# Gathers of a graph network written out with constant counts and without a wait for their landing

## What is computed

```python
h = jnp.maximum(_layernorm(x, axis=-1), 0.0)
msg_input = jnp.concatenate([h[src], h[dst], edge_attr], axis=-1)
m = jax.nn.relu(msg_input @ Wm1 + bm1)
messages = jax.nn.relu(m @ Wm2 + bm2)
agg = jax.ops.segment_sum(messages, dst, num_segments=N)
u = jax.nn.relu(jnp.concatenate([h, agg], axis=-1) @ Wu1 + bu1)
out = x + h + (u @ Wu2 + bu2)
```

## Time and profile before

| | us |
|---|---|
| median of 3 runs | 946.89 |
| lowest and highest run | 946.84, 947.41 |
| the profiled execution | 952.33 |
| its span (first to last instruction) | 950.6 |
| GpSimd busy in it | 566.0 |
| gathers (L246), 392 of them | 386.1 |

### The profile page before, as it was taken

One profiled execution on the slowest core, in us unless ns is written; L12 is line 12 of the kernel. 1 busy time (PEld: TensorE's weight loads), 2 busy tenths in 40 slices (PEclk: granted clock), 3 DMA queues, 4 the chain that ended last, 5 costly groups with the idle time before them and its releaser, 6 DMA issues. The chain is left out here.

```text
span 950.6 us, 19507 instructions
## 1 busy us (share of the span) xinstructions
PE 751.0 (79%) x3158; PEld 453.1 (48%) x3159; DVE 696.0 (73%) x2407; ACT 608.5 (64%) x1384; POOL 566.0 (60%) x829
## 2 busy tenths in 40 slices
PE   0687768767877778877887776886799999999998
PEld 0344334333433334433443433453457788777776
DVE  3866756666677666776667567766499999998887
ACT  0666556556656565665665566655567788988986
POOL 6656655656566555665556555654198766655453
PEclk9988888889789897889887899988899999999999
DMA  6254445445545455545553454447305799999999
GB/s 158 67 178 158 151 154 175 157 127 178 176 157 168 141 176 165 169 148 161 177 176 129 153 176 155 162 150 232 133 12 176 230 319 335 351 341 349 355 360 328
DMA packets 99726, 184.55 MB, mean 194 GB/s; under 512 B 15101, under 2 KB 16512, under 8 KB 99700
## 3 DMA queue, kind: packets, MB, share of 16 engines
q1 hardware_dynamic: 46084, 80.64, 25.4%
q10 hardware_dynamic: 41072, 77.93, 23.5%
q0 software_dynamic: 12544, 25.72, 10.5%
HBM read 107.25 MB, written 76.98 MB: 194 GB/s over the span
## 5 line engine op out<-in xcount | busy, mean ns | idle before, releaser
L246 POOL DMA_INDIRECT xg<-x_in,ends_now x392 | 386.1, 985 | 142.9 <-issue 130.1
L511 PE MATMUL bank<-ht,w_uh 128*128 128x512 f32 x196 | 146.1, 837 | 114.2 <-ACT ht L441 68.8
L644 POOL TENSOR_TENSOR low<-msgs,high 128x128 fp32r<-128x128 f32 x303 | 152.8, 521 | 73.3 <-ACT high L724 70.1
L309 DVE BATCH_NORM_STATS2 bn<-xg 128x6 f32<-128x128 f32 x392 | 80.6, 278 | 132.4 <-DMA xg<-x_in,ends_now 132.3
L673 DVE TENSOR_SCALAR hot<-node,dst_f,minus_base 128x512 fp32r<-128x512 f32 x229 | 131.2, 616 | 23.2 <-issue 16.3
L777 PE MATMUL bank<-hot,low 128*128 128x512 f32 x303 | 136.4, 450 | 12.2 <-POOL low L644 6.5
L429 ACT ACTIVATE zn<-xn,shift,rstd 128x128 f32<-128x128 f32 x343 | 141.6, 483 | 1.6 <-DVE rstd L348 1.2
L511 PEld LDWEIGHTS bank<-ht,w_uh 128*128 128x128 f32 x196 | 42.6, 249 | 199.6 <-issue 180.1
L436 ACT ACTIVATE ht<-bank 128x512 f32<-128x512 f32 x196 | 109.2, 593 | 30.3 <-PE bank L504 26.1
L778 PE MATMUL bank<-hot,high 128*128 128x512 f32 x303 | 120.8, 399 | 0.0
L504 PE MATMUL bank<-ident,xg 128*128 128x128 f32 x392 | 64.8, 298 | 61.1 <-issue 37.0
(11 more groups left out here) (77 smaller groups left out, 1165.7 us busy)
## 6 DMA issues: line engine op xcount, KB each, us to landing
hu_scratch<-ht ACTq DMA_DIRECT2D x49, 512.0 KB
xh_scratch<-xh_o ACTq DMA_DIRECT2D x49, 512.0 KB
hu_i<-hu_scratch SPq DMA_DIRECT2D x98, 256.0 KB
xh_i<-xh_scratch SPq DMA_DIRECT2D x98, 256.0 KB
out<-xh_o SPq DMA_DIRECT2D x97, 256.0 KB, 4.3
xn<-x_in ACTq DMA_DIRECT2D x44, 512.0 KB
xg<-x_in,ends_now POOLq DMA_INDIRECT x392
edge<-edge_t_in ACTq DMA_DIRECT2D x45, 64.0 KB
```

The source lines that it names most:

```text
L246: pool.indirect_dma_start(xg[:, slot, t, :], None, x, bass.IndirectOffsetOnAxis(ap=ends_now[:, slot8, t:t + 1], axis=0)).then_inc(s_xg[slo ...
L511: pe.matmul(p_hu[:], w_uh[:], ht[:, slot % 2, 2 + n, :], start=True, stop=True).then_inc(s_hus, 1)
L644: return pool.tensor_tensor(low[:, at, :], msgs[:, k, :], high[:, at, :].bitcast(F32), ALU.subtract)
```

## The change

The loop over the steps on GpSimd becomes 49 steps written out, so that every wait has a constant count and every gather reads its eight index columns straight from `ends_all`. The ring `ends_now`, its copies and their semaphore are gone. Of the three waits of a step one is left, for the transposes of the slot's last user, with the same count as before (4(s - 3) - 2 = 4(s - 4) + 2). The wait for the landing of the step before is gone. Instead, each gather posts `s_made` when GpSimd has written its descriptors (`engine_sem`), and gather n waits for that of gather n - 3 (`AHEAD = 3`).

```diff
--- before.py
+++ after.py
@@ -24,6 +24,7 @@
 EPS = 1e-5
 STAT = 12
 TABLE = 18
+AHEAD = 3
 assert GROUPS == 2 * STEPS and (NEW - LAST) % 4 == 0
 
 
@@ -92,7 +93,7 @@
         s_rng = sem("ranges_moved")
         s_xn = [sem(f"nodes_loaded{i}") for i in range(4)]
         s_xg = [sem(f"ends_gathered{i}") for i in range(4)]
-        s_cp = sem("ends_copied")
+        s_made = sem("gathers_issued")
         s_stat = sem("stat")
         s_sd = sem("sd_ready")
         s_zv = sem("z_by_vector")
@@ -133,7 +134,6 @@
         with ExitStack() as one:
             ident = sb("ident", [P, P], on=one)
             ends_all = sb("ends_all", [P, STEPS, 8], I32, on=one)
-            ends_now = sb("ends_now", [P, 8, 8], I32, on=one)
             dst_i = sb("dst_i", [P, ET + SPARE], I32, on=one)
             minus_i = sb("minus_i", [P, GROUPS], I32, on=one)
 
@@ -227,31 +227,24 @@
                 pool.memset(ident[:], 0.0).then_inc(s_cst, 1)
                 pool.memset(msgs[:, ET:, :], 0.0).then_inc(s_cst, 1)
                 pool.wait_ge(s_idx, 16)
-                pool.tensor_copy(ends_now[:, 0:4], ends_all[:, 0:4, :]).then_inc(s_cp, 1)
-                pool.wait_ge(s_cp, 1)
-
-                def body(s, slot8, use8):
-                    slot = slot8 % 4
-                    if at_least(s, 4):
-                        pool.wait_ge(s_tr, 4 * (s - 3) - 2)
-                    if at_least(s, 1):
-
-                        pool.wait_ge(s_xg[(slot8 - 1) % 4], 128 * (2 * use8 + (slot8 - 1) // 4 + 1))
-                    if at_least(s, 4):
-                        pool.wait_ge(s_cp, 8 * use8 + slot8 - 2)
-                    if below(s, STEPS - 4):
-                        pool.tensor_copy(ends_now[:, (slot8 + 4) % 8, :], ends_all[:, s + 4, :]
-                                         if isinstance(s, int) else ends_all[:, bass.ds(s + 4, 1), :]).then_inc(s_cp, 1)
+
+                for s in range(STEPS):
+                    slot, use = s % 4, s // 4
+                    if s >= 4:
+                        pool.wait_ge(s_tr, 4 * (s - 4) + 2)
                     for t in range(8):
+                        n = 8 * s + t
+                        if n >= AHEAD:
+
+                            pool.wait_ge(s_made, n - AHEAD + 1)
                         pool.indirect_dma_start(
                             xg[:, slot, t, :], None, x,
-                            bass.IndirectOffsetOnAxis(ap=ends_now[:, slot8, t:t + 1], axis=0)).then_inc(s_xg[slot], 16)
-                    if not at_least(s, 1):
+                            bass.IndirectOffsetOnAxis(ap=ends_all[:, s, t:t + 1], axis=0), engine_sem=s_made
+                            ).then_inc(s_xg[slot], 16)
+                    if s == 0:
                         pool.wait_ge(s_cst, 6)
                         pool.affine_select(out=ident[:], in_=ident[:], compare_op=ALU.not_equal, fill=1.0, base=0,
                                            pattern=[[-1, P]], channel_multiplier=1).then_inc(s_cst, 1)
-
-                run_steps(pool, STEPS, 8, STEPS - 4, 8, body)
 
             def start_table(dve, did):
```

## The result

The changed kernel took 977.63 us (median of 4 runs, 973.80 to 985.41) beside 947.15 us for the kernel before: 1.033 times the time, 95% interval 1.0267 to 1.0395. Forecast were 939.9 us and a range of 929 to 960. The profiled execution took 976.8 us, span 975.1.

The account below looks back on a forecast made before the run. The loop through ScalarE's second relu, the node load's issue and L320 was taken to set the step's length in stage one. Terms -3.1 - 14.1 + 10.2 = -7.0 us gave 946.9 - 7.0 = 939.9 us, range 929 to 960.

Parts of the forecast that it names:

- No wait for landing: GpSimd's gathers no longer wait for the previous step's landing: start gains 3.1 us, seven long steps 14.1 us.
- the slower rival: From L174's issue to L320, each node load slows by 1.0 us a step: +22.8, 969.7 us; chance 0.15.
- The seven long steps: Steps that gathers end, L309 running straight into L320; expected to fall back to the load's 4.0 us: -14.1 us.
- The gathers at the load's start: Gather bursts move to the node load's issue; one gather delays each of some 40 loads by 0.255 us: +10.2 us.
- The new wait: On GpSimd, each gather waits for the descriptors of gather n - 3; priced at zero.
- the straight code: GpSimd's loop written out; a late instruction fetch costs some us once, with four steps of cover: priced at zero.
- the indices: Indices read in place: 45 copies of 187 ns leave GpSimd; priced at zero, 8.4 us together without cover.
- gathers bind: Within a rival: waits costing over 0.3 us on GpSimd; every 0.1 us more is 39 us; chance 0.08 shared with another case.
- 3.2 us "to spare": GpSimd's slack per step: eight gathers take 10.3 us of a 13.5 us step.
- Even sharing of the DMA engines: Rival: engines serve gather and load queues in turn, +0.5 us a step on the load: +2.8, 949.7 us; chance 0.15.

Follow-up runs that it names:

- the one with two slots: Changed kernel, but gathers wait for the transposes of step s - 2 instead of s - 4: 910.2 us (chip 6), 904.0 (chip 0), 963.8 (chip 14).

## Why the prediction was wrong

**The step that failed is "No wait for landing".** It priced the start at -3.1 us. On the first chip it was +23.7 (step 3 at 82.38 instead of 58.70). I asked what the wait holds up, and found two idle stretches of L309. I did not ask what the wait keeps apart: it was also the only break in GpSimd's issue, and on such chips VectorE and TensorE need one. The trace of before had a hint: signals some tenths of a us late at the end of its runs. Neither the sum nor any rival held such a case; the slower rival put the loss in the node loads, of which none became slow.

**The terms in the steady part were about right against the trace they were read from.** The seven long steps went: none of 42 loads takes over 4.6 us to L313, against seven before, worth about 14 us. The gathers at the load's start cost 4.14 - 3.99 = 0.15 us each, 6 us in all, against 0.255 and 10.2 forecast. But a third term was missing: ScalarE's second relu starts 9.22 us after L313 instead of 9.01, since the transposes wait 1.31 us for their input's signal instead of 0.53; over 44 steps that is 9 us. -14 + 6 + 9 = +1, as measured between the two profiled executions. The -14 itself was partly luck of that trace: it was read from an execution 5.4 us over the median and applied to the median too, and with the landing wait put back one step was long, not seven, and the steady part 9 us shorter. The new wait, the straight code (21 instruction packets) and the indices cost nothing, as priced; that was shown by putting back the landing wait alone.

**What the late signals cost in all** is seen between chips, in the same kernel: step 48 starts at 687.4 us on the first and 614.2 on chip 0. Of these 73 us, 27 stand before step 3, and 46 after it, 1.0 us a step, of which the second relu (it starts 9.22 against 8.28 us after L313) has 0.94. That the rest of the two chips is alike is assumed here.

**Where no signal is late, the sign was right and the size was not.** The start gained 3.2 us (58.27 to 55.10) for 3.1 forecast. Yet the gain is 63 us, not 7, because there gathers end 31 of 42 steps in the kernel before, not seven: a step falls from 13.84 to 12.46 us. In the forecast that stood only as "gathers bind", for another reason. That a trace of one chip says seven and of another thirty-one could not be read from the one at hand; that the margin was thin could: eight gathers of 10.1 us, 2.4 of landing and 0.9 to the next start are 13.4, against a step of 13.5. I had called 3.2 us "to spare" without setting the landing against it.

**Even sharing of the DMA engines** was priced at 0.5 us more for each load. It was 0.15, with one to two gathers beside each. Even sharing is the rule of the Trainium skill (DMA: Bandwidth & Descriptors, Queues, rings and completion order) that the prediction weighed; the trace agrees with it in sign only.

## What to carry to other kernels

Before a wait is removed, ask what it separates as well as what it delays: look at what the other engines do in the longest stretch that becomes unbroken, and break a long run of gathers on purpose. Add up the chain that a wait closes (issue, landing, next start) and set it against the period; if the two are equal, the wait binds even when a second wait behind it seems to cover it. Time a change on more than one chip when it alters how densely something is issued: here one edit gave 1.033 and 0.934. Three versions were run on both sorts of chip in full: the changed kernel, the one with two slots, and the one with a 3 us break of constant writes in the middle of each step. Only the last beats the kernel before on both (0.993 and 0.965); where signals are not late, the changed kernel itself is better (0.934).

## What was unexpected of the hardware

Chips came in two sorts for this kernel. On chips 5, 14 and 3, and on the one of the first result, the kernel before takes 944 to 948 us, and signals of VectorE and TensorE are late while gathers are issued, by up to 21.9 us (a run of 24). On chips 6, 0 and 7 it takes 971 to 973 us, and none is late, even in runs of 88 and 112 gathers. No chip had a second turn, so whether this belongs to the chip or to the time at which it was used is not shown. Independent vector statistics are spaced out too (1.1 us of idle before each at 39 us, with nothing to wait for), so it is not the signal alone that is held up. The traces differ in one more way. Where signals are late, 15 to 50% of the semaphore events of TensorE, VectorE and ScalarE are missing in stage one. On chips 6, 0 and 7 they are there (on chip 0, 954 events for the 949 of VectorE in the changed kernel), and so they are in stage two on every chip. Every execution of the changed kernel that is timed here was also recorded with its clock, so whether signals are late without the recording is not shown.

The delay does not hang on the bytes (half of them: the same); that it hangs on the descriptors which GpSimd writes fits the runs, but their number was not varied by itself.

The cause stays open. The Trainium skill names one place where GpSimd and VectorE can hold each other up, a shared pair of SBUF ports (SBUF — State Buffer, SBUF: two separate sides), and says that TensorE and ScalarE never wait for anyone there. ScalarE's signals agree, never late; TensorE's do not, being the latest of all. Nor does that rule know two sorts of chip. What differs between the chips, and why landings take 0.4 us longer where signals are in time, no run here shows.
